# Six sequences in flight instead of four, one tile for queries, keys, probabilities and outputs, and a new order of the steps

## The reference

```python
# each block: h = ln(x) * (1 + scale) + shift ; x = x + f(h)
# attention, 16 heads:
sim  = einsum('bhnd,bhmd->bhnm', q, k) * scale
attn = softmax(sim); out = einsum('bhnm,bhmd->bhnd', attn, v) @ wo + bo
# layer 0: heads of 64, q and k rotated by position, gelu feed forward      ("rope", "rope", "ff")
# layer 1: heads of 8, gelu (tanh form)                                    ("small", "small", "ff")
# layer 2: heads of 64, gated gelu                                         ("flat", "flat", "ff")
# layer 3: heads of 8, q and k normalized per head, sums gated, gated silu ("small", "small", "ff")
```

## Time and profile before

| | |
|---|---|
| median of 3 runs | 1689.47 us (1688.17 to 1692.95) |
| profiled execution | 1690.91 us, its span 1688.9 us |
| busy, share of the span | PE 90%, DVE 83%, ACT 65%, POOL 54% |
| granted TensorE clock, mean | 0.970 of full speed |

### The profile page before, as it was taken

The page is one execution under the profiler, slowest core; times in us unless marked ns, Lnnn a source line. Parts: engine busy times, 40 slices in busy tenths (PEclk is TensorE's granted clock), DMA queues, the critical chain, the costliest instruction groups (busy, mean ns, idle before and its releaser), DMA issues.

```text
span 1688.9 us, 40850 instructions
## 1 busy us (share of the span) xinstructions
PE 1518.5 (90%) x15228; PEld 1196.7 (71%) x15228; DVE 1403.1 (83%) x3745; ACT 1095.0 (65%) x4765; POOL 911.7 (54%) x1028
## 2 busy tenths in 40 slices
PE   6988999999889989999988989999989999989875
PEld 5876777677667777777766767776767778767653
DVE  5878788988997778898898868998898888888864
ACT  1766778657565777756576667766666686775632
POOL 3746454555765546455566646545575664554432
PEclk9999999999999999999999999999999999999975
DMA  9100000000000000000000000000000000000000
GB/s 328 37 1 2 2 2 2 7 4 4 7 8 2 2 1 2 2 7 7 6 3 7 2 2 2 2 7 1 7 7 7 2 2 2 2 2 3 3 1 3
DMA packets 14437, 20.91 MB, mean 12 GB/s; under 512 B 4064, under 2 KB 10784, under 8 KB 14240
## 3 DMA queue, kind: packets, MB, share of 16 engines
q1 hardware_dynamic: 14240, 18.31, 3.3%
HBM read 17.25 MB, written 1.05 MB: 11 GB/s over the span
## 4 chain that ended last, share of the span: by engine, by line
PE 47%; DVE 38%; POOL 8%; ACT 5%; issue 2%; DMA 0%; SPq 0%; POOLq 0%; ACTq 0%; DVEq 0%
DVE negmax L1007 9%; PE ps L665 9%; PE ps L691 6%; PE ps L552 6%; PE ps L704 5%; POOL E L859 5%; DVE E L1108 4%; ACT E L752 4%; DVE xn L967 3%; PE ps L678 3%; DVE E L1060 3%; PE ps L629 3%; PE ps L643 2%; PE ps L576 2%; PE ps L567 2%; PE ps L655 2%
## 5 line engine op out<-in xcount | busy, mean ns | idle before, releaser
L752 ACT ACTIVATE E<-ps,negmax 128x128 f32<-128x128 f32 x2048 | 719.3, 410 | 261.9 <-DVE negmax L1007 249.4
L859 POOL TENSOR_TENSOR E<-E,rinv 128x512 f32<-128x512 f32 x512 | 525.2, 1042 | 375.3 <-DVE rinv L1016 373.2
L752 ACT ACTIVATION_READ_ACCUMULATOR E<-ps,negmax 128x1 f32 x2048 | 509.7, 250 | 0.0
L1007 DVE TENSOR_REDUCE negmax<-ps 128x4 f32<-128x512 f32 x512 | 330.1, 680 | 59.3 <-PE ps L629 33.8
L665 PE MATMUL ps<-consts,E 128*128 128x128 f32 x2048 | 316.8, 285 | 39.7 <-POOL E L859 24.1
L1108 DVE COPY E<-ps 128x512 f32<-128x512 f32 x448 | 299.8, 678 | 54.6 <-PE ps L665 52.4
L665 PEld LDWEIGHTS ps<-consts,E 128*128 128x128 f32 x2048 | 233.0, 144 | 116.0 <-POOL E L859 67.6
L852 POOL TENSOR_TENSOR E<-E,prod 128x512 f32<-128x512 f32 x128 | 162.3, 1274 | 73.9 <-DVE prod L1063 72.2
L807 POOL TENSOR_TENSOR rstd<-ve,consts 128x1 f32<-128x1 f32 (+1 forms) x192 | 107.9, 563 | 83.5 <-DVE ve L960 74.0
L691 PE MATMUL ps<-E,VV 128*64 128x128 f32 x2048 | 139.4, 282 | 2.2 <-DVE E L1108 2.1
L761 ACT ACTIVATE VV<-ps 128x512 f32<-128x512 f32 x128 | 77.3, 671 | 89.8 <-PE ps L567 89.5
(11 more groups left out here) (130 smaller groups left out, 2757.1 us busy)
## 6 DMA issues: line engine op xcount, KB each, us to landing
w_f<-res_f SPq DMA_DIRECT2D x6, 256.0 KB, 11.5
qT<-in_x SPq DMA_DIRECT2D x16, 64.0 KB, 1.8
w_wq<-res_wq SPq DMA_DIRECT2D x2, 512.0 KB, 7.8
w_wk<-res_wk SPq DMA_DIRECT2D x2, 512.0 KB, 8.4
w_wv<-res_wv SPq DMA_DIRECT2D x2, 512.0 KB, 9.1
w_wo<-res_wo SPq DMA_DIRECT2D x2, 512.0 KB, 9.8
w_cq<-res_cq SPq DMA_DIRECT2D x2, 512.0 KB, 10.8
w_co<-res_co SPq DMA_DIRECT2D x2, 512.0 KB, 13.7
```

The source lines that it names most:

```text
L752: last = nc.scalar.activation(E[p][:, h, :], bank(u, j * N, (j + 1) * N), ACT.Exp, bias=negmax[p][:, h:h + 1], accum_out=sums[p][:, h:h + 1])
L859: tt(e, e, rinv[p][:, T4 * g:T4 * g + T4].unsqueeze(2).broadcast_to([N, T4, N]), ALU.mult).then_inc(done[POOL], 1)
L1007: nc.vector.tensor_reduce(negmax[p][:, T4 * g:T4 * g + T4], bank(u).rearrange("p (h m) -> p h m", h=T4), AX, ALU.max, negate=True).then_in ...
```

## The change

There are three parts. First, `STREAMS` is 6. Second, `qT` and `kT` are gone: queries, keys, probabilities and outputs of a block share `E[p]`, the small things move into corners of `E` and `VV`. The instructions stay the same in number, kind and size, only their addresses change. Third, `schedule()` is rewritten: costs are finer; going from one tiling of the array to another costs time on PE (`switch`); PE work is slowed by a modelled half clock (`Clock`); each engine has its own candidate, ranked by `way`, the age of the sequence, and two tables (`FAVOUR`, `TURN`); the table `KEEP` says how many banks a step must leave free (0 where it has no row); and the scores may not run further ahead of ScalarE than `AHEAD`.

```diff
-STREAMS = 4
+STREAMS = 6
...
-REACH = {PE: 0.25, DVE: 0.13, ACTE: 0.2, POOL: 0.1}
-TABLE_LOAD = 1.3
-REFILL = 0.1
-AGE = 30.0
-SPARE = 2
-OWN = ("PV", "PJ", "D", "O0", "O1")
...
+TAIL = {PE: 0.16, DVE: 0.08, ACTE: 0.13, POOL: 0.04}
+SIGHT = {PE: 0.06, DVE: 0.04, ACTE: 0.04, POOL: 0.085}
+FIRST_STEP = 21.0
...
[...]
+ENTER_TILED = {"row32": 0.094, "row64": 0.094, "col32": 0.12, "col64": 0.1}
+LEAVE_TILED = {"row32": 0.1, "row64": 0.1, "col32": 0.114, "col64": 0.151}
+AGE = 16.8
+TURN = [0, 0, 0, 0, 0, 0, 0, 0, -3, 0, 14, 0, 0, 0, 0, 14]
+AHEAD = {"small": 5.4, "rope": 2.3}
+FAVOUR = {
+    (POOL, "RQ", "rope"): 62, (POOL, "power", "flat"): -8, (POOL, "prob", "small"): -2, (POOL, "xb", "ff"): -64,
...
+KEEP = {
+    (PE, "C", "small"): 2, (PE, "CT", "rope"): 1, (PE, "HC", "small"): 1, (PE, "K", "flat"): 2,
...
-            add(PE, f"MX{g}", 0.45, (e, f"PT{g}"), (DVE, "V"), *([(PE, f"MX{g - 1}")] if g else []),
+            add(PE, f"MX{g}", 0.242, (e, f"PT{g}"), (DVE, "V"), *([(PE, f"MX{g - 1}")] if g else []),
...
+def tiling_of(key):
+    engine, step, b, _ = key
+    if step[0] == "S":
+        return "row64" if KIND[b] == "flat" else "row32"
+    return "col32" if step[:2] == "MX" else "col64" if step[0] == "O" else "whole"
+def switch(old, new):
+    if old == new:
+        return 0.05 if old == "col64" else 0
+    return LEAVE_TILED.get(old, 0) or ENTER_TILED.get(new, 0)
...
+    rank = {key: way[key] - AGE * key[3] + FAVOUR.get(kind_of(key), 0) + TURN[key[3]] for key in cost}
...
+                if n:
+                    if len(open_) - n < keep[key]:
+                        continue
...
+                if ahead[key] is not None:
+                    t = max(t, free[ACTE] - ahead[key])
+                able = free[e]
+                if e == PE:
+                    able += switch(array, tiling[key])
...
+                if port[key] and pool_from <= start < pool_to:
+                    start = pool_to + PORT_SWITCH
+                score = (start, -rank[key], index[key])
...
+        free[e] = clock.run(start, cost[key]) if e == PE else start + cost[key]
+        end[key] = free[e] + TAIL[e]
...
-        qT = each("qT", 128, H // 2, N)
-        kT = each("kT", 128, H // 2, N)
...
-        xin = [qT[p][:, 0, :] for p in range(STREAMS)]
+        xin = [E[p][:, 12, :] for p in range(STREAMS)]
...
+        gates = [VV[p][:, 512:896] for p in range(STREAMS)]
+        small_q = [E[p][:, 0, :] for p in range(STREAMS)]
+        small_k = [E[p][:, T4:2 * T4, :] for p in range(STREAMS)]
...
-                            last = mm(bank(unit, j * N, (j + 1) * N), qT[p][p0:p0 + DH, t, :],
-                                      kT[p][p0:p0 + DH, t, :], start=True, stop=True)
+                            q, k0 = (T4 * GROUP[f"{n}{t // T4}"] + t % T4 for n in "QK")
+                            last = mm(bank(unit, j * N, (j + 1) * N), E[p][p0:p0 + DH, q, :], E[p][p0:p0 + DH, k0, :],
+                                      start=True, stop=True)
...
-                    nc.scalar.activation(qT[p][:, T4 * i:T4 * i + T4, :], bank(u).rearrange("p (t n) -> p t n", t=T4),
+                    nc.scalar.activation(E[p][:, 2 * T4 * i:2 * T4 * i + T4, :], bank(u).rearrange("p (t n) -> p t n", t=T4),
```

More of the change, by code:

```diff
@@ L188, in table_of, with waits_for_port, kind_of, __init__ @@
     return {2: "gelu", 5: "gelu_tanh", 8: "gelu"}.get(b, "exp")
+def tiling_of(key):
[7 more added lines that the diff above has]
+    return LEAVE_TILED.get(old, 0) or ENTER_TILED.get(new, 0)
+def waits_for_port(key):
+    return key[0] == DVE and key[1] in ("norm", "squares", "factors", "heads")
+def kind_of(key):
+    engine, step, b, _ = key
+    return engine, step if step in ("U0", "U1") else step.rstrip("0123"), KIND[b]
+class Clock:
+    def __init__(self):
+        self.busy, self.halved = [0.0] * 4000, [True]
+    def is_halved(self, w):
+        while len(self.halved) <= w:
+            share = self.busy[len(self.halved) - 1] / WINDOW
+            self.halved.append(share < (BUSY_FROM if self.halved[-1] else IDLE_BELOW))
+        return self.halved[w]
+    def run(self, t, work):
+        while work > 1e-12:
+            w = int((t + PHASE) / WINDOW)
+            speed = 1 / HALVED if self.is_halved(w) else 1
+            until = (w + 1) * WINDOW - PHASE
+            can = (until - t) * speed
+            if can >= work:
+                self.busy[w] += work / speed
+                t += work / speed
+                work = 0
+            else:
+                self.busy[w] += until - t
+                work -= can
+                t = until + 1e-9
+        return t
 def schedule():
@@ L215, in schedule @@
         stack.pop()
-    order = {e: [] for e in (PE, DVE, ACTE, POOL)}
-    free = {e: 0.0 for e in order}
+    index = {key: i for i, key in enumerate(cost)}
+    rank = {key: way[key] - AGE * key[3] + FAVOUR.get(kind_of(key), 0) + TURN[key[3]] for key in cost}
+    keep = {key: KEEP.get(kind_of(key), 0) for key in cost}
+    tiling = {key: tiling_of(key) for key in cost}
+    table_for = {key: table_of(key) for key in cost}
+    port = {key: waits_for_port(key) for key in cost}
+    ahead = {key: AHEAD.get(KIND[key[2]]) if key[0] == PE and key[1][0] == "S" else None for key in cost}
@@ L219, in schedule @@
+    turning = {key: KIND[key[2]] == "rope" and key[0] == DVE and key[1] in ("Q0", "Q1", "K0", "K1") for key in cost}
+    order = {e: [] for e in ENGINES}
+    free = {e: FIRST_STEP for e in ENGINES}
     vacant = {i: 0.0 for i in range(BANKS)}
-    end, bank_of, table = {}, {}, "exp"
+    end, bank_of, table, array = {}, {}, "exp", "whole"
+    pool_from = pool_to = 0.0
+    turned, added = 0, []
+    clock = Clock()
     left = {key: len(after[key]) for key in cost}
-    ready = [key for key in cost if not left[key]]
+    ready = {e: [] for e in ENGINES}
@@ L258, in schedule @@
             if not left[user]:
-                ready.append(user)
-    assert len(end) == len(cost)
+                make_ready(user)
     return order, bank_of, fills, max(end.values())
@@ L1082, in step_of @@
                     if b == 4:
[L1083 removed]
+                        tt(small_k[p], keys, own, ALU.mult).then_inc(done[DVE], 1)
                     else:
[L1085 removed]
+                        stt(out=small_k[p], in0=keys, scalar=v("bk1" if b == 3 else "bk3"), in1=own,
                             op0=ALU.add, op1=ALU.mult).then_inc(done[DVE], 1)
```

240 lines of the change are left out of this document (132 added, 108 removed).

## The result

| | before | after |
|---|---|---|
| median of the runs | 1689.18 us (4 runs) | 1552.89 us (1551.32 to 1557.72, 4 runs) |
| ratio, 95% interval | | 0.9194 [0.9168, 0.9220] |
| span of the profiled execution | 1688.9 us | 1552.5 us |

What follows compares the result with a forecast made beforehand. No engine binds alone; the end hangs on how TensorE's and VectorE's nearly full lists interlock. Terms -41 - 70 - 17 - 12 - 20 + 2 = -158 us gave 1531 us, range 1450 to 1600.

Steps and rivals of the forecast that it cites:

- Tilings: TensorE's order: 392 fewer changes of tiling at 0.105 us each, 41 us gained, bounds 12 and 59.
- Idle time of the body: TensorE's idle time with four sequences in flight, 120.9 us, falls by 0.42 to 51, a gain of 70 us.
- the prediction's own sign: Body window of TensorE: idle some 3 to 4% if right, near 8% again if the waits stay.
- What goes with a wait: Some 0.17 us counted busy before each of TensorE's 178 body waits: 17 us gained, bounds 0 and 30.
- Half clock in the body: Short half-clock stretches of the body, 46 us, half of it lost: 12 us gained, bounds 0 and 23.
- The tail: Last 547 matmuls, as sequences run out: 113 us against 131, 20 us gained, bounds 0 and 35.
- The start: Six more SyncE transfers ahead of bias rows and weights: 2 us lost, bounds 0 and +4.
- The rule on the shared port: VectorE and GpSimd lock a shared SBUF port: denser GpSimd work costs VectorE a few us more.
- The drain rule: Changing tiling mode drains TensorE: a bare drain of 0.17 us would make the tilings term 67 us, not 41.
- Waits that stay: Rival: eight PSUM banks carry six sequences, only tilings, tail and a little clock gain: 1626 us, chance 0.13.
- four-bank scores: Rival: rope and small scores needing four banks at once wait for exponentials, 96 steps: 1733 us, chance 0.04.
- Nearly no waits: Rival: TensorE runs almost without waits, body idle falls by 111 us: about 1450 us, chance 0.21.

Runs made afterwards that it cites:

- the added changes: Changed kernel, same order, a one-column 32-column-tiling matmul before each of 192 transposes of x: 1583.17 us; control with whole-array matmuls: 1575.33 us.
- the second neighbour: Changed kernel with the planner's AGE at 16.7 in place of 16.8, nothing else: 1598.74 us, ratio 0.9467.
- tuned_six: Changed kernel with four planner costs corrected by its trace, tables and AGE picked by some 50,000 planner trials: 1542.57 us, ratio 0.9125.
- near_order: Changed kernel with the planner's AGE at 16.81 in place of 16.8: 1604.42 us, ratio 0.9494.
- tuned_four: Changed kernel's planner and costs with four sequences, tables picked for four by about 50,000 planner trials: 1631.06 us, ratio 0.9662.
- six_old_order: Changed kernel with six sequences and the common tile, but the planner and constants of before: 1666.42 us, ratio 0.9865.
- four_new_order: Changed kernel with STREAMS = 4, costs and tables as in the change: 1703.17 us, ratio 1.0086.
- old_order_tilings: Kernel before, four sequences and old planner, which now also counts a cost for a change of tiling: 1749.48 us, ratio 1.0355.

## Why the prediction was right, and where it was off

*The mechanism* held: time went from waits, tilings, half clock and the tail at once, and the homes cost nothing. That the sum came within 22 us is partly luck: idle time and what goes with it fell short by some 50 us, while tilings, tail, half clock and changes of line, which the sum doesn't have, gave some 37 more than forecast.

*Tilings* were forecast at 41 us and came out at 58 by the timeline. 0.105 us a change was read from one tiling; over all 797 places it is 0.136, part of which any change of line costs. The runs show both limits of such a price: the added changes cost little, 334 changes fewer under the old planner made the kernel slower, and the second neighbour has one change of tiling more than the change, 500, and is 46 us slower. As a share of TensorE's list the upper bound of the prediction, 59, was the right one; as a price at the end of the program it isn't shown.

*Idle time of the body* is the step that failed: 70 us forecast, 27 measured (119.5 to 92.7 over equal work). The counts of chains that are longer than the work beside them pointed the right way; the mistake was to scale idle time by about VectorE's 0.40. Idle time fell to 0.78. The step from three to four in flight doesn't give it either: with the cuts put right the idle share with three is 6.5 / 61.4 = 10.6%, the step is 0.75, and two such steps leave 0.56. By the prediction's own sign, 3 to 4% idle if right and near 8% if the waits stay, the 6.5% is nearer to the rival. The sum of that missing time over TensorE and VectorE is of more use if it is set against the whole time and not against the idle part. Counted in the same way for every order that ran:

| kernel | missing time in the order, us | end by the planner, us | measured, us |
|---|---|---|---|
| corrected costs, tables for six (tuned_six) | 140 | 1507 | 1543 |
| the change | 148 | 1518 | 1553 |
| `AGE` 16.81 (near_order) | 186 | 1574 | 1604 |
| `AGE` 16.7 (near_order_b) | 201 | 1570 | 1599 |
| tables for four (tuned_four) | 252 | 1607 | 1631 |
| six, old planner (six_old_order) | 265 | 1649 | 1666 |
| before | 332 | 1676 | 1689 |
| four, new planner (four_new_order) | 345 | 1668 | 1703 |
| old planner told of tilings (old_order_tilings) | 387 | 1758 | 1749 |

From first to last 247 us of missing time go with 206 us of the measured, 0.83 to one, and only one pair of neighbours is out of order. It seems to hold clock and waits in one. The slope is read from these same runs, so 184 x 0.83 = 153 us for the change is hindsight and no forecast; a straight line through all nine has 0.77. The third column does at least as well: there the fixed lists of each kernel are played through with the corrected costs of tuned_six. It too has one pair of neighbours out of order, the kernel before and four_new_order, and sets the change 158 us under the kernel before where 136 were measured. With its own uncorrected costs the changed planner gives 149 us (1639.9 against 1490.7).

*What goes with a wait* was 17 forecast and 10 measured, in line with waits that stayed. *Half clock in the body*, 12 forecast, 15 measured. *The tail*: 20 forecast, 29 measured. The forecast stands on the misread cuts. The counts 547, 256 and 87 belong to the true ends, so these 547 matmuls took 149.7 us before and not 131, and a matmul cost 61.4 / 291 = 0.21 us with three in flight, 46.8 / 169 = 0.28 with two and 41.5 / 87 = 0.48 with one, and in the body 1514.2 / 8173 = 0.185. The same sum with these costs is 302 x 0.185 + 136 x 0.21 + 101 x 0.28 + 8 x 0.48 = 117 us, a gain of 33. The new tail took 121.1 us, where the prediction's sign asked for about 110; part of the difference is a stretch of 35 us with three sequences left at a clock of 0.81, where three ran at full clock before.

*The start*, +2 forecast. SyncE asks for the bias rows at 12.60 us, as worked out, and GpSimd's first addition (line 969) starts at 21.59. The timeline of TensorE:

```profile
26.45 0.94 PE L643 MATMUL ps<-consts,xn 128*128 128x128 f32 x2 [9.27 <-DVE cn L1102]
```

GpSimd's first addition starts as before, so the transfers stayed hidden. The first transpose is at 26.45 in place of 23.96, because VectorE and GpSimd now do the statistics of more sequences before the first `norm`: 2.5 us, the number right and the cause another.

The rule on the shared port (the Trainium skill, SBUF — State Buffer, section SBUF: two separate sides) spoke for longer normalizations:

```profile
L1100 DVE TENSOR_SCALAR xn<-X,mv,rstd x176: 307/337/1420, 83.2 to 1543.1; 128x128 f32<-128x128 f32 x176
```

The median is 337 ns against 341, with a maximum of 1420, and the mean of the page went from 503 to 423. The loss got smaller, not larger. Of the 192 normalizations 71 took over 450 ns before, and 69 of these began while a GpSimd operation ran; now 28 do. It is the planner's doing and not that of the number in flight, since 72 do with six sequences under the old planner. The planner of the change holds such a step back until GpSimd's operation is over, which is the likely reason; no run has that rule alone. The lock doesn't catch every meeting, as 33 of the 121 short ones before also began during a GpSimd operation. The drain rule (the Trainium skill, TensorEngine Tiling (Array Packing), section Key Properties), with the row's 0.17 us for a drain, would have given 67 us where 58 came; the 0.01 and the 0.15 us of leaving show that no one figure stands for it.

*The rivals.* Waits that stay (1626) and four-bank scores (1733) did not come; the wait of the small scores for exponentials up to 1440 us was 4.5 us on five occasions, that of the rope scores 0.9 us on two. Nearly no waits (1450) did not come either, and no order tried came near it. Which share of the near_order gap is waits and which is the clock's answer to them isn't settled by a run of its own; no kernel here has the one without the other.

## What to carry to other kernels

When no engine binds alone, price an order as a whole, and not by what one saving is worth: by the work that it puts beside each chain, summed over the full engines, or by playing its fixed lists through a cost model. Compare such ends only for orders that really run. Treat a list order that a search has picked as a thing of its own: run neighbours of it before you credit the idea behind it, and search again after every change of a cost. More items in flight and a better order paid together here: 23 and 58 us alone, 136 together. And when many rows of one line look alike, count them through the order before you call one the end of a sequence.

## What was not expected

A change of 0.01 in one constant of the planner moved the kernel by 52 us, five times what a corrected cost model and a new search gained, and the planner's own end had 48 of them. Leaving a tiling cost 0.15 us behind value products and 0.01 behind a one-column matmul. Removing 96 us of work from an engine that is busy 88% of the span gave 16 us.
